# A planned attention and ternary-FFN kernel: four groups of input transfers leave the head of SyncE's queue, chunk one's normalization waits for chunk zero, and the planner's tie seeds are drawn anew

## What is computed

```
x: 1 x 2048 x 256, f32
xn = (x - mean) / sqrt(var + 1e-5)                     # over the last axis
out = x + attention(xn) + ffn(xn)

attention(xn):                                         # 8 heads of 32, 2 key/value heads, causal
    q, k, v = xn@Wq, xn@Wk, xn@Wv;  q, k = rope(q), rope(k)
    std = softmax(q k^T / sqrt(32)) v
    geo = softmax(outer(q[:3].dir, k[:3].dir)) v       # dir: one unit vector for each head
    o = std + head_scales * (geo - std);  return o @ Wo

ffn(xn):                                               # 1024 hidden, ternary weights
    tq(W) = clip(round(W / mean|W|), -1, 1) * mean|W|
    z = xn @ tq(W_syn).T + b_syn
    hidden = relu(z) where z >= the 102nd largest of its row, else 0
    return layernorm(xn + hidden @ tq(W_out).T + b_out) * gamma + beta
```

## Time and profile before

| | |
|---|---|
| median of 3 runs | 722.5 us (721.86 to 723.41) |
| the profiled execution | 720.07 us, of which the span of the trace is 718.3 |
| busy share of the span | PE 93%, PEld 44%, DVE 70%, ACT 62%, POOL 33% |
| mean granted TensorE clock | 0.974 |
| data moved | 30.81 MB by DMA |

### The profile page before, as it was taken

One profiled execution on the slowest core, in us unless ns is written; L12 is line 12 of the kernel. 1 busy time (PEld: TensorE's weight loads), 2 busy tenths in 40 slices (PEclk: granted clock), 3 DMA queues, 4 the chain that ended last, 5 costly groups with the idle time before them and its releaser, 6 DMA issues. The chain is left out here.

```text
span 718.3 us, 12337 instructions
## 1 busy us (share of the span) xinstructions
PE 666.0 (93%) x4424; PEld 318.5 (44%) x4424; DVE 501.0 (70%) x976; ACT 448.7 (62%) x732; POOL 234.5 (33%) x312
## 2 busy tenths in 40 slices
PE   3779889999899999998999999998999999999997
PEld 2443444434534434343444434444445364555543
DVE  7866988587668666677776766776677767567922
ACT  5525556353775443467754543479989999898762
POOL 6433355312323230123100211303643353444653
PEclk9978989999999989999999999999999999999999
DMA  8577000001720000016000000000100010000000
GB/s 244 194 188 205 16 10 30 0 2 41 204 46 2 1 1 0 1 61 152 1 6 1 1 1 1 1 18 30 38 24 23 24 31 21 25 24 8 9 1 30
DMA packets 26194, 30.81 MB, mean 43 GB/s; under 512 B 7105, under 2 KB 21313, under 8 KB 25746
## 3 DMA queue, kind: packets, MB, share of 16 engines
q1 hardware_dynamic: 24210, 29.45, 14.6%
q10 hardware_dynamic: 1920, 0.54, 0.3%
HBM read 17.72 MB, written 11.53 MB: 41 GB/s over the span
## 5 line engine op out<-in xcount | busy, mean ns | idle before, releaser
L944 ACT ACTIVATE probs<-scores 128x1024 f32<-128x1024 f32 (+3 forms) x320 | 271.2, 895 | 207.7 <-PE acc L1490 155.4
L1181 DVE TENSOR_REDUCE piece_max<-side 128x1 f32<-128x512 f32 x190 | 126.8, 686 | 49.1 <-PE side L1380 47.4
L1483 PE MATMUL acc<-probs,v_nat 128*32 128x512 f32 (+3 forms) x1280 | 151.2, 545 | 2.6 <-POOL probs L788 2.0
L1490 PE MATMUL acc<-probs,ones_all 128*32 128x512 f32 (+3 forms) x1280 | 151.3, 545 | 0.0
L1380 PE MATMUL side<-k_stack,q_stack 128*128 128x512 f32 (+3 forms) x317 | 123.1, 438 | 9.0 <-DMA q_stack<-q_parked 2.4
L788 POOL TENSOR_SCALAR_AFFINE_SELECT probs<-probs 128x256 f32<-128x256 f32 x128 | 56.6, 452 | 206.2 <-ACT probs L944 205.3
L1380 PEld LDWEIGHTS side<-k_stack,q_stack 128*128 128x128 f32 x317 | 55.5, 192 | 99.8 <-DVE piece_max L1181 37.1
L1465 PE MATMUL scores<-q_stack,k_stack 128*128 128x512 f32 (+3 forms) x320 | 91.2, 389 | 5.1 <-ACT probs L944 3.9
L1184 DVE CUSTOM_DVE_ANT_0 side<-side,tail_mask 128x128 f32<-128x128 f32 (+3 forms) x127 | 62.2, 497 | 31.5 <-PE side L1380 30.8
L1465 PEld LDWEIGHTS scores<-q_stack,k_stack 128*128 128x128 f32 x320 | 54.0, 194 | 33.0 <-ACT probs L944 24.2
L1483 PEld LDWEIGHTS acc<-probs,v_nat 128*32 128x32 f32 x1280 | 34.2, 110 | 67.8 <-issue 54.2
(11 more groups left out here) (170 smaller groups left out, 893.6 us busy)
## 6 DMA issues: line engine op xcount, KB each, us to landing
q_stack<-q_parked SPq DMA_DIRECT2D x12, 512.0 KB, 7.2
q_parked<-turned SPq DMA_DIRECT2D x8, 512.0 KB, 3.4
res<-in_L_attn_x_dram SPq DMA_DIRECT2D x4, 512.0 KB, 6.1
x_parked<-xn SPq DMA_DIRECT2D x4, 512.0 KB, 3.2
xT_parked<-xnT SPq DMA_DIRECT2D x4, 512.0 KB, 2.9
xz<-xT_parked SPq DMA_DIRECT2D x16, 128.0 KB, 2.5
xb<-x_parked SPq DMA_DIRECT2D x16, 128.0 KB, 2.0
out_dram<-res SPq DMA_DIRECT2D x16, 128.0 KB, 1.7
```

Of the source, the lines that this page charges most:

```text
L944: nc.scalar.activation(probs[:, slot % 2, pair, :, off:], scores[:, pair, :, off:], ACT.Exp, scale=ATT_SCALE if kind == 0 else 1.0).then_i ...
L1181: free(nc.vector.tensor_reduce(piece_max[:, h, p:p + 1], pt, AX.X, ALU.max), ("S",) + a)
L1483: nc.tensor.matmul(acc[D * h:D * h + D, 0, off:], v_nat[:, j, g], probs[:, slot_no[a] % 2, h // 2, h % 2, off:], start=(j == 0), stop=(j = ...
L1490: last = nc.tensor.matmul(acc[D * h:D * h + D, 1, off:], ones[:, 0:D], probs[:, slot_no[a] % 2, h // 2, h % 2, off:], start=(j == 0), stop ...
```

## The change

Three things are edited.

1. On SP, the loads of x chunks 2 and 3, of W_syn, and of the "late" group (Wo, head scales, four bias and gain vectors) leave the head of the queue and become planned pieces of the flow `stack`, behind chunk 0's stacks and geometric transfers. The geometric transfers of chunk 0 go into that flow too, so they now come behind the stacks. Their arrival is modelled (LANDING) rather than given.
2. Chunk 1's `shift` waits for `rope 0 K`, and chunk 1's `xn` for `hi 0`.
3. All 29 seeds are new.

```
-           "stack_lo": 8000, "xz_in": 2300, "xb_in": 2300}
+           "stack_lo": 8000, "x": 5000, "late": 4000, "w_in": 6000, "xz_in": 2300, "xb_in": 2300}
-SEEDS = (2, 0, 26, 34, 44, ...
+SEEDS = (5, 31, 0, 2, 8, ...
-        add("stat", "dve", STAT_RANK if c else 0, ("shift", c), 180, [("rstd", c)])
+        add("stat", "dve", STAT_RANK if c else 0, ("shift", c), 180, [("rstd", c)] + [("rope", 0, "K")] * (c == 1))
-            add("norm", "act", 1, ("xn", t), 400, [("shift", c)] + [("unit", "xT", c - 1, 1), ("xn_park", c - 1)] * (c > 0))
+            add("norm", "act", 1, ("xn", t), 400, [("shift", c)] + [("hi", 0)] * (c == 1) + [("unit", "xT", c - 1, 1), ("xn_park", c - 1)] * (c > 0))
-        add("geo", "sp", 1, ("geo_rows", c, 1), 3300, [("geo_lo", c), ("geo_hi", c)] + used)
-        add("geo", "sp", 1, ("geo_dma", c), 2200, [("geo_top", c)] + used)
+        add("geo" if c else "stack", "sp", 1, ("geo_rows", c, 1), 3300, [("geo_lo", c), ("geo_hi", c)] + used)
+        add("geo" if c else "stack", "sp", 1, ("geo_dma", c), 2200, [("geo_top", c)] + used)
+        if c == 0:
+            for n in (2, 3):
+                add("stack", "sp", 1, ("x", n), 500)
+            add("stack", "sp", 1, ("w_in", 0), 500)
+            add("stack", "sp", 1, ("late",), 4000)
-    done = {("x", 0): 5200.0, ("x", 1): 13000.0, ("x", 2): 19000.0, ("x", 3): 21000.0, ("ang_in", 0): 9500.0, ("dir_in",): 14000.0}
-    done.update({("w",): 11000, ("late",): 26000, ("w_in", 0): 18000, ("w_in", 1): 19000})
+    done = {("x", 0): 5200.0, ("x", 1): 10000.0, ("ang_in", 0): 9500.0, ("dir_in",): 14000.0}
+    done.update({("w",): 11000})
...
-            sp.dma_start(w_raw.rearrange("p (a n) -> p a n", a=NN),
-                         W_syn.rearrange("(a p) n -> p a n", p=P)).then_inc(up_in, 16)
-            for c in range(2, NCH):
-                sp.dma_start(res[:, TPC * c:TPC * c + TPC], x_rows[c]).then_inc(x_in[c], 16)
-            sp.dma_start(w_o[:], Wo.rearrange("(g p) n -> p g n", p=P)).then_inc(late_in, 16)
...
             for key in plan["sp"]:
                 k = key[0]
+                if k == "x":
+                    c = key[1]
+                    sp.dma_start(res[:, TPC * c:TPC * c + TPC], x_rows[c]).then_inc(x_in[c], 16)
+                if k == "w_in":
+                    sp.dma_start(w_raw.rearrange("p (a n) -> p a n", a=NN),
+                                 W_syn.rearrange("(a p) n -> p a n", p=P)).then_inc(up_in, 16)
+                if k == "late":
...
```

9 lines of the change are left out of this document (5 added, 4 removed).

## The result

The changed kernel takes 726.42 us in the median of 7 runs (724.83 to 730.19), the kernel before beside it 721.89 us (716.61 to 723.41, 7 runs). The ratio is 1.0079, 95% interval 1.0049 to 1.0110: slower by 5.7 us by the ratio, 4.5 by the two medians. Forecast were 720.5 us and faster; the range of 716.5 to 725.5 does not hold it either. The profiled execution took 726.99 us with a span of 725.2, against 718.3 before.

A forecast was written before the change was run, and what follows sets the result against it. PE, busy for 666.0 of 718.3 us, was taken as the bound, with its pauses and halved clock. Terms -0.6 - 1.3 - 0.9 + 1.1 + 0 - 1.5 + 1.2 = -2.0 took the median 722.5 to 720.5 us; range 716.5 to 725.5.

The forecast's parts named there:

- Chunk 1's projections: PE's start of chunk 1's projections: 40.35 us against 40.95, a gain of 0.6 us (bounds -2.0 and +3).
- the second rival: Clock low for all of chunk 1's projections, so slower or the same: 722.5 us, at most 723.5; chance 0.14.
- The wait for the geometric maxima: PE's 1.31 us wait at 51.13 us, before the geometric scores, disappears: -1.3 us (bounds -1.3 and 0).
- the low clock at 51.20 to 54.70: Half-clock stretch on PE: -1.7 us at full clock, 0 if it falls anyway; the middle, -0.9, was taken.
- DVE up to `m`: DVE's reductions start earlier, 4.5 us gained, against 4.1 lost to W_syn's cut before `m`: 0 (bounds -1.5 and +3).
- W_syn's work on PE: W_syn's transposes and sum move into PE's busy row-maxima stretch, partly filling the pause around `m_dma`: +1.1 us (0 to +2.8).
- the low clock from 89.20 on: Low clock to 95.80 us, behind the `m_dma` pause, shortens from 6.6 to about 3.5 us: -1.5 us (-3.2 to 0).
- The seeds: Nine more mode changes on PE cost +1.2 us; the new draw's other effects taken as 0, 3 us either way.
- The prediction's own sign for the seeds: Start as forecast, but the stretch after 110 us longer or shorter by more than 3 us: seeds decide, not transfers.
- The first rival: W_out's 1 MB load ahead of `m_dma` delays the first standard scores: 724.0 us, 725.5 at full price; chance 0.22.
- The third rival: A lucky draw of ties cuts low clock and pauses after 110 us: 4 us more gained, 717 us; chance 0.14.
- the fourth: Rival: the start gains 3 us, but FFN and attention take it back, so 722.5 us; chance 0.10.

The follow-up runs named there:

- new_start: Joined order: the changed kernel's code and order up to near 182 us, then the kernel before's order for what is left; 730.66 us, ratio 1.0118.
- head_swap: Changed kernel with the moved loads at the head of SP's list again and POOL's cut ahead of the spread again; 723.26 us, ratio 1.0027.
- pause: Kernel before with one edit: POOL's cut placed behind the spread of chunk 2, as in the changed kernel; 724.57 us, ratio 1.0047.
- late_two: Kernel before with the loads of x 2 and 3, w_o and the small vectors moved behind chunk 0's stacks; 735.02 us, ratio 1.0171.
- old_start: Joined order: the kernel before's order and transfers up to near 170 us, then the changed kernel's order; 719.41 us, ratio 0.9988.
- late_split: Kernel before with x 2 and 3, w_o and small vectors loaded behind chunk 0's stacks, DVE's split of `b_up` behind chunk 0's `m`; 720.80 us, 1.0006.
- swap: Changed kernel with POOL's cut moved ahead of the spread of chunk 2 again; 724.82 us, ratio 1.0043.
- head: Changed kernel's orders kept, the moved loads issued at the head of SP's queue as in the kernel before; 726.34 us, ratio 1.0083.
- old_50: Joined order: the kernel before's order and transfers up to near 50 us, then the changed kernel's order; 721.47 us, ratio 1.0016.

## Why the prediction was wrong

*Chunk 1's projections, -0.6.* They start at 41.25 against 40.95 (forecast 40.35): +0.3, within the bounds. POOL's table copies, which were to begin near 33.9, began at 36.03 (35.27 before). The clock in 40 to 48 us is 0.71 against 0.72 before, so the second rival did not happen. Its price was a little low: 7.14 us with 3.2 of them at the lower level would be 11.1 at 1.2 GHz throughout, not 10.

*The wait for the geometric maxima, -1.3; the low clock at 51.20 to 54.70, -0.9.* Right, and better than said. PE after:

```profile
49.96 0.51 PE L1477 MATMUL scores<-q_geo,k_geo 32*128 32x512 f32 x4
...
51.54 1.02 PE L1377 MATMUL side<-turned,dirs_q 128*40 128x512 f32 x2
```

No wait, the clock is 1.00 from 48 to 60 us (0.86 before), and the first reduction starts at 50.77 (50 to 52 was said). That no wait is left owes something to luck: new_start, with the same order up to there, waits 1.17 us for these maxima and starts its scores at 49.94, so the data land about then.

*"DVE up to `m`", 0; W_syn's work on PE, +1.1; the low clock from 89.20 on, -1.5.* Here the prediction failed. The 10.6 us at the standard scores are three differences:

- The last reduction comes 2.8 us late (84.31 against 81.53). The reductions did start 4.6 us sooner, as forecast, but took 33.5 us instead of 26.1: among them now lie the pause of 4.61 us and the low clock behind it. In head_swap, which has no such pause, the last reduction is at 76.88, and the gain of 4.7 comes through.
- From there to the issue of `m_dma` it is 5.9 us against 2.5, 3.4 more. 5.7 was said: the cut between `mx` and `m` was well sized.
- From the issue to the scores it is 7.7 us against 3.3, 4.4 more, where nothing was said. This is where W_syn's transposes stand.

So "DVE up to `m`: 0" took the move of 3.64 us of DVE from 27 to 85 us as a matter of DVE's free time alone. It puts the two instructions of the cut beside POOL's copies, mix and cuts, and these are on PE's path: 3.39 us of wait, and a second low stretch. The transposes, which were to fill the pause around `m_dma`, stand behind that wait, and with it between PE and the scores. PE after:

```profile
94.52 1.11 PE L1415 MATMUL side<-ident,h_split 128*128 128x128 f32 x4 [1.03 <-ACT up_T L985]
...
96.31 1.97 PE L1415 MATMUL side<-ident,h_split 128*128 128x128 f32 x8 [0.68 <-ACT up_T L985]
```

PE begins them at 92.38 at half the clock, with two waits for ACT's copies between them, and comes to the scores at 97.93. +1.1 (at most 2.8) was said for them. Windows after, to be held against the one low stretch of before:

```profile
92.00:96.00 4.00, 2.61 (x24) 1.60 (x16) 1.98 (x6) 2.28 (x5) 0.43 (x1) 0.54 0.27 110
96.00:100.00 4.00, 3.69 (x17) 3.36 (x17) 4.00 (x5) 2.25 (x4) 0.00 (x0) 0.60 0.11 32
...
108.00:112.00 4.00, 4.00 (x22) 2.07 (x22) 3.96 (x6) 1.20 (x2) 2.34 (x2) 0.50 0.05 15
```

*A term that is missing.* The one cause that has a price of its own isn't in the sum at all: POOL's cut behind the spread, 3.4 us alone (pause). The prediction follows POOL only for the table copies near 34 us; the exchange stood in its list, some 25 us later.

*The seeds, +1.2 with 3 us either way.* A late start is partly made up for. In the profiled executions, from the standard scores to the last `o`, the changed kernel wins back 3.7 us of 10.6, pause 3.3 of 4.7, late_two 3.5 of 17.9 and new_start 3.3 of 9.0, the last three with before's seeds behind 170 us. By these the new draw regains no more than the old one. The ratios, which rest on 6 to 12 executions each, say otherwise: of 10.6 us the changed kernel has 5.7 left, pause 3.4 of 4.7, late_two 12.3 of 17.9, new_start 8.5 of 9.0 (its profiled execution was 3.3 us faster than its median). new_start differs from the changed kernel in the rest alone, and is 2.8 us slower with intervals that overlap. So "0" for the rest of the draw is not shown: with a late start the new draw may give back some 3 us, with an early one it gives less than 2.8 (old_start). The prediction's own sign for the seeds, more than 3 us behind 110 us, was meant for a start as forecast, and the start was not. The 9 changes of mode (+1.2) were not tried by themselves. What the seeds and edits 1 and 2 did decide together is the start, by the exchange on POOL and the place of W_syn's cut.

*The first rival*, W_out's load ahead of `m_dma`, came nearest (725.5 at full price), and by luck, since its reason did not happen. SP and PE after, and a window with its DMA share (the last but one number):

```profile
88.78 0.40 SPq L722 DMA_DIRECT2D z_buf<-in_L_ffn_W_out_dram  x1
90.20 1.46 SPq L628 DMA_DIRECT2D q_stack<-maxima  x2
...
97.93 1.20 PE L1473 MATMUL scores<-q_stack,k_stack 128*128 128x512 f32 x2
...
93.50:95.50 2.00, 0.98 (x4) 0.71 (x4) 1.48 (x5) 0.96 (x3) 0.00 (x0) 0.50 0.00 0
```

No wait of the standard scores for a transfer is shown, and there was none: from 93.50 to 95.50 the DMA engines moved nothing, so the maxima, issued at 90.20, had been moved by 93.5 although 1 MB was issued ahead of them. That is the 3.3 us of before and not the 9.3 that the rival and the sentence on the shared engines in the prediction take for a small transfer behind a large one. The scores start behind the transposes, which ended last. The third rival (a lucky draw) and the fourth (nothing arrives) fall with the interval.

*What is shown and what isn't.* Shown: the loss is in the first 170 us (old_start, new_start); in before's order the loads of x 2 and 3, w_o and the vectors are free (late_split); in before's order the exchange on POOL costs 3.4 us (1.5 to 5.2, pause), against 5.7 for the whole change. Shown as a mechanism, not as a price: POOL and DVE hold each other at W_syn's cut. By subtraction (swap's 0.43% against before) what is left beside the exchange is 3.1 us (0.9 to 5.3), and that takes with it whatever else the new start does; head against old_50 gives up to 4.8. The parts are not shown to add up. Open: why head is no faster than the changed kernel, with a first pause 3 us shorter and a start 4.8 us earlier, which speaks against the exchange's price holding in the changed order; and edit 2 and the move of W_syn's load, which no run tries alone.

## What to carry to other kernels

When an order is redrawn, compare it on every engine, the one at 33% too: a short instruction placed behind one that waits for a transfer stops the engine that is the bound, and costs its wait plus the low clock behind it. When an instruction of DVE that reads two tiles in SBUF moves, or another beside which POOL was seen to be held, look at what GpSimd does at the new place, since each of the two can be held while the other works. And before one moves a load, list all its consumers in their engines' orders: 4 KB for a bias cost 12 us (late_two).

## What the runs showed of the hardware that was not expected

A POOL instruction beside one of DVE's two instructions of a weight cut, or beside its split of `b_up`, was held until that one ended, wherever this document shows one: copies of 180 ns took up to 2331 ns (DVE's instruction 2350), two cuts of 0.90 took 3.59, a copy of 0.29 took 1.27. It holds the other way too: DVE's 2.35 us became 3.24 beside a POOL mix, and 1.30 became 2.19. Length isn't what does it: before, DVE's reciprocal of 3.35 us (77.11 to 80.46, one input) ran beside two of POOL's cuts at 79.11, and they took their usual 0.90 us. The Trainium skill states this in "SBUF — State Buffer" ("SBUF: two separate sides"): VectorE and GpSimd share a port pair as "an exclusive lock, not a bandwidth split", for VectorE instructions in a mode with two ports, or with two inputs in SBUF against a GpSimd instruction that reads SBUF. The trace agrees with the lock, and with the second condition: the instruction of 2.35 us reads `z_buf` and `h_split`. The one of 1.29 us has one input, and a copy beside it took 1237 ns; it handles the same 2048 columns in 1286 ns against 2350, which would fit such a mode, but no row names it. I had not weighed that rule in the prediction, and it was the one that spoke against the change.

Of TensorE's clock: behind the pause of 4.61 us the granted clock was 0.50 and 0.52 (1.2 GHz) for the next 8 us, though PE was busy for all of them; behind the 3.20 us of pause it was 0.50 for the same 8 us. Windows of before, the changed kernel and pause, in this order:

```profile
64.00:76.00 12.00, 11.28 (x68) 4.81 (x68) 9.30 (x33) 5.07 (x8) 3.51 (x8) 0.86 0.48 100
64.00:76.00 12.00, 11.77 (x74) 4.95 (x66) 7.45 (x29) 3.22 (x6) 3.66 (x8) 0.67 0.61 131
64.00:76.00 12.00, 11.27 (x60) 5.13 (x56) 7.40 (x30) 1.33 (x3) 2.79 (x7) 0.65 0.47 97
```

PE is about as busy in all three. In full clock that is (0.86 - 0.65) x 12 = 2.5 us lost in pause, on top of its wait of 3.20 us, and 2.3 us in the changed kernel, on top of 4.61.
